# Moving the expert part's tiles in SBUF by unused tiles of 32 to 96 bytes, in a decoder layer on one Trainium2 core

## What is computed

```python
router_probs = softmax(x @ w_router)
gate_weights = softmax((x @ w_gating) / GATE_TEMP)
g = einsum('bsh,ehf->ebsf', x, w_gate)      # E=8 experts, H=256, F=1024
u = einsum('bsh,ehf->ebsf', x, w_up)
h = silu(g) * u
expert_out = einsum('ebsf,efh->ebsh', h, w_down)
cw = router_probs * gate_weights
cw = cw / (cw.sum(-1) + 1e-09)
out = einsum('ebsh,bse->bsh', expert_out, cw)
x = layernorm(x + out)
```

## The kernel before

| tile | before | rem. 256 | after | rem. 256 |
|---|---|---|---|---|
| xh, xl (tokens) | 57984, 72320 | 128 | same | 128 |
| wh0, wl0 | 86656, 98944 | 128 | 86720, 99008 | 192 |
| acc | 111232 | 128 | 111296 | 192 |
| wh1, wl1 | 127584, 139872 | 96 | 127744, 140032 | 0 |
| sil0, sil1, hf0, hf1 | 152160 to 158304 | 96 | 152320 to 158464 | 0 |
| hh0, hl0 | 160352, 176736 | 96 | 160544, 168736 | 32 |
| hh1, hl1 | 168544, 184928 | 96 | 176960, 185152 | 64 |
| xk | 193120 | 96 | 193344 | 64 |

## Time and profile before

### The profile page before, as it was taken

One profiled execution on the slowest core, in us unless ns is written; L12 is line 12 of the kernel. 1 busy time (PEld: TensorE's weight loads), 2 busy tenths in 40 slices (PEclk: granted clock), 3 DMA queues, 4 the chain that ended last, 5 costly groups with the idle time before them and its releaser, 6 DMA issues. The chain is left out here.

```text
span 1966.1 us, 25813 instructions
## 1 busy us (share of the span) xinstructions
PE 1807.1 (92%) x9624; PEld 1491.7 (76%) x9624; DVE 1329.3 (68%) x2421; ACT 842.5 (43%) x1327; POOL 2.6 (0%) x22
## 2 busy tenths in 40 slices
PE   2399999999999987888789999999999999999997
PEld 1277777777777775555579988989988889898986
DVE  6889999999999952899864444454444454454445
ACT  2466677666667733222243333232333232333333
POOL 0000000000000000000000000000000000000000
PEclk9689999999999998889779999999999999999999
DMA  3000001001001002112020101000000000002001
GB/s 107 0 27 17 6 27 38 6 6 43 17 12 48 1 0 66 64 31 60 10 74 33 33 1 33 33 32 32 32 0 32 32 32 32 32 2 67 1 1 38
DMA packets 35648, 56.98 MB, mean 29 GB/s; under 512 B 2997, under 2 KB 20850, under 8 KB 35058
## 3 DMA queue, kind: packets, MB, share of 16 engines
q1 hardware_dynamic: 35570, 55.95, 8.8%
HBM read 52.27 MB, written 3.67 MB: 28 GB/s over the span
## 5 line engine op out<-in xcount | busy, mean ns | idle before, releaser
L1424 DVE TENSOR_TENSOR hf<-sil,fbanks 128x512 f32<-128x512 f32 (+1 forms) x128 | 79.4, 621 | 338.1 <-PE fbanks L1593 278.7
L1532 ACT ACTIVATE sil<-fbanks 128x512 f32<-128x512 f32 (+1 forms) x128 | 69.6, 544 | 448.7 <-PE fbanks L1593 448.7
L1609 PE MATMUL fbank<-wl,hh 128*128 128x256 f32 x896 | 251.9, 281 | 0.0
L1609 PE MATMUL fbank<-wh,hl 128*128 128x256 f32 x896 | 251.8, 281 | 0.0
L1609 PE MATMUL fbank<-wh,hh 128*128 128x256 f32 x896 | 251.8, 281 | 0.0
L1424 DVE TENSOR_TENSOR hf<-sil,fbank 128x512 f32<-128x512 f32 (+1 forms) x128 | 79.6, 621 | 154.2 <-PE fbank L1593 147.0
L725 PE MATMUL pair<-wcv,kf 128*112 128x256 f32 x768 | 176.2, 379 | 0.0
L1609 PEld LDWEIGHTS fbank<-wl,hh 128*128 128x128 f32 x896 | 170.1, 190 | 2.1
L1609 PEld LDWEIGHTS fbank<-wh,hh 128*128 128x128 f32 x896 | 170.0, 190 | 2.0
L1609 PEld LDWEIGHTS fbank<-wh,hl 128*128 128x128 f32 x896 | 170.2, 190 | 0.0
L1431 DVE TENSOR_TENSOR hl<-hf,hh 128x512 fp32r<-128x512 f32 (+1 forms) x256 | 158.3, 618 | 0.0
(11 more groups left out here) (220 smaller groups left out, 3452.2 us busy)
## 6 DMA issues: line engine op xcount, KB each, us to landing
raw<-in_w_gate SPq DMA_DIRECT2D x16, 512.0 KB, 3.7
raw<-in_w_up SPq DMA_DIRECT2D x16, 512.0 KB, 4.7
raw<-in_w_down SPq DMA_DIRECT2D x16, 512.0 KB, 5.6
raw<-in_w_ck SPq DMA_DIRECT2D x4, 1024.0 KB, 4.9
wcv<-in_w_cv SPq DMA_DIRECT2D x4, 768.0 KB, 4.5
raw<-in_ctx_t SPq DMA_DIRECT2D x4, 750.0 KB, 5.3
ct<-in_ctx_t SPq DMA_DIRECT2D x4, 750.0 KB, 4.9
x<-in_x SPq DMA_DIRECT2D x4, 448.0 KB, 6.6
```

The source lines that it names most:

```text
L1424: dve.tensor_tensor(hf[i][:, 0:w], sil[i][:, 0:w], bank[2 * i + 1][:, 0:w], ALU.mult).then_inc(hf_ready, 1)
L1532: act.activation(sil[f % 2][:, 0:w], bank[2 * (f % 2)][:, 0:w], ACT.Silu).then_inc(sil_ready, 1)
L1609: ins = pe.matmul(bank[4 + 2 * (t % 2) + i // 2][:, (i % 2) * C:(i % 2 + 1) * C], a[t % 2][:, f, i * P:(i + 1) * P], m[h][:, DOWN + f * C: ...
```

## The change

Four tiles that nothing reads or writes are allocated between the others, and hl0 is allocated before hh1. Every instruction stays. With `gap_w0` (64 bytes) the weights of half 0 stand at +64 from the tokens by the remainder of 256, with `gap_w1` (96 bytes) those of half 1 at +128. `gap_h0` and `gap_h1` (32 bytes each) put hh0 and hl0 32 bytes past a multiple of 64 and hh1 and hl1 on one. Counting the loaded tile's remainder minus the streaming tile's:

| matmuls | before | after |
|---|---|---|
| gate and up, half 0 | 0 | +64 |
| gate and up, half 1 | -32 | +128 |
| down, half 0, even and odd steps | -32, -32 | +96, +128 |
| down, half 1, even and odd steps | 0, 0 | +32, +64 |

```diff
@@ -1283,11 +1283,15 @@
         top, total, rec = (sb(n, [P, 2 * TILES]) for n in ("ltop", "ltotal", "lrec"))
         cw = sb("cw", [P, E, TILES])
         cws, cwr = sb("cws", [P, TILES]), sb("cwr", [P, TILES])
+        sb("gap_w1", [P, 24])
         wh, wl = g["wh"] + [sb("wh1", [P, WH], F32R)], g["wl"] + [sb("wl1", [P, WH], F32R)]
         sil = [sb(f"sil{i}", [P, COLS]) for i in range(2)]
         hf = [sb(f"hf{i}", [P, COLS]) for i in range(2)]
-        hh = [sb(f"hh{i}", [P, FB, COLS], F32R) for i in range(2)]
-        hl = [sb(f"hl{i}", [P, FB, COLS], F32R) for i in range(2)]
+        sb("gap_h0", [P, 8])
+        hh, hl = ([sb(f"{n}0", [P, FB, COLS], F32R)] for n in ("hh", "hl"))
+        sb("gap_h1", [P, 8])
+        hh.append(sb("hh1", [P, FB, COLS], F32R))
+        hl.append(sb("hl1", [P, FB, COLS], F32R))
         xk = sb("xk", [P, TILES, C])
@@ -1654,6 +1658,7 @@
         rwkv_phase(nc, g, io)
         g["xh"], g["xl"] = (ctx.enter_context(nc.sbuf_tensor(n, [P, CB, N], F32R)) for n in ("xh", "xl"))
+        ctx.enter_context(nc.sbuf_tensor("gap_w0", [P, 16], FP32))
         g["wh"], g["wl"] = ([ctx.enter_context(nc.sbuf_tensor(n, [P, WH], F32R))] for n in ("wh0", "wl0"))
         g["acc"] = ctx.enter_context(nc.sbuf_tensor("acc", [P, TILES, C], FP32))
```

## The result

The changed kernel takes 1967.38 us (median of 20 runs, 1965.52 to 1972.71), the kernel before 1963.37 us (20 runs beside them, 1960.82 to 1969.80). The ratio is 1.0017, with a 95% interval of 1.0009 to 1.0024: slower by 0.17%, where 7 us less was forecast. 1967.4 us lies inside the range, on the wrong side of the time before.

What follows compares the result with a forecast made beforehand. TensorE's matmul pace was taken to bound the expert part. Terms of -7.2, +0.9, -2.4 and +1.8 us summed to -6.9, so 1964.2 became 1957.3 us, with a range of 1944 to 1970 us.

Steps and rivals of the forecast that it cites:

- What bounds the kernel: Expert part: its 941.6 us are TensorE's alone, shortened only by the pace at which matmuls follow each other.
- That the place of one operand against the other sets the pace: Expert matmuls: loaded tile's place against the streaming tile's sets the surcharge of 10 to 20 ns per matmul.
- That it is a cost of two reads at once: Expert matmuls: the next weights' load and the stream read SBUF together; the 10 to 20 ns surcharge is their mutual cost.
- the reading by remainder of 64: Gate, up and down: distances priced as multiples of 64 or off them, -6.9 us in sum; chance 0.42.
- The slower rival: Half 0 loses distance 0: gate/up at 233.3 ns, down 119.8 everywhere, +7.2 and +4.2 us, 1966 to 1976 us; chance 0.18.
- the bursts of six: First part's 256-column channel matmuls, 112 weights: 118 ns at 0, 114 at -128 (+128 by 256), 120 at +64; left out of sum.
- Nothing moves: Expert part: halves differ by something other than distance, such as region, so the time stays at 1964 us; chance 0.20.
- Down: Down matmuls: half 1's even steps gain 2.4 us, half 0's odd steps lose 1.8, the other steps keep their price.
- Part 3: Everything behind gap_w0 moves by 64 to 224 bytes; costed at nothing in the attention part and hidden in the expert part.
- the prediction's own sign: Rows up to 1011.7 us should keep their times within a microsecond or two, else the costing of moved tiles is wrong.

Runs made afterwards that it cites:

- zero_both: Kernel before with tiles moved so weights stand at distance 0 from the tokens and down at -32 in both halves; 1952.44 us, ratio 0.9947.
- w0_back: Changed kernel without gap_w0 and with gap_w1 of 40 elements, so half 0's weights return to distance 0 from the tokens; expert part 942.3 us.
- all_moved: Kernel before with all tiles 64 bytes further, distances by remainder of 256 as before, hl0 allocated before hh1; expert part 941.3 us.
- short_loads: Kernel before with 64 of 128 weight columns in the middle four of each six gate/up matmuls; 512 tokens took 228.9 and 232.1 ns (halves 0, 1).
- short_32: Kernel before with 32 of 128 weight columns in the middle four of each six gate/up matmuls; 512 tokens took 230.6 and 232.1 ns (halves 0, 1).
- the map: Table over several kernels that differ in tile places, weights -96 to +128 bytes from tokens; gate/up with 512 tokens 227.2 ns at 0, 234.1 at +96.
- zero_256: zero_both with gap_w1 of 72 elements in place of 8, so everything from wh1 on stands 256 bytes further; expert part 931.0 us.
- last_64: zero_both with the last 256 tokens 48 elements further in xh and xl, putting weights at +64 from them; 1951.11 us, ratio 0.9943.
- last_down_64: last_64 with hh and hl of both parities at +64 from the weights instead of -32; expert part 928.8 us.

## Why the prediction was wrong

*What bounds the kernel* held. The expert part is TensorE's alone, and its length moved the total one to one: +4.1 us gave +4.0 in the medians, and in zero_both -10.2 us (-9.3 in the second profile, with the later rise of the clock) gave -10.2.

*That the place of one operand against the other sets the pace* held, and is shown: w0_back, zero_both, all_moved. *That it is a cost of two reads at once* was argued only, and its plain form, a price for each column that the load reads, is refuted at 512 tokens by short_loads and short_32. Whether the start of a load has a part in it wasn't tried.

*The failed step is the reading by remainder of 64*: "The nearest reading is by remainder of 64, since 0 and -32 are the two classes that rows 5 tell apart." Two points were made into two classes, and +64 and +128 were priced by them. Of the twelve distances in the map nine cost 232 to 234 ns, and the kernel before had in half 0 the cheapest of all. Moving half 1 from -32 to another distance was worth 0.8 us instead of 7.2, and moving half 0 away from 0 cost 7.1 instead of nothing. Those two terms are 6.4 + 7.1 = 13.5 us of error; the 256-token steps gave back 2.3 us in half 0 and 0.6 in half 1, and down added 0.5, which leaves, but for rounding, the 11.0 us between -6.9 and +4.1. (The prediction's product 6.2 x 1152 is 7.1; its 7.2 is that of the unrounded paces.)

*The slower rival* came nearest: "0 against not 0 by a remainder over 64". Its +7.2 us for half 0 was measured as +7.1. Of its 11.4 us 4.1 came, since it had +4.2 us for down, where the sum of the four terms is -0.1, and nothing for the 256-token steps of half 0 (-2.3) and the 512-token steps of half 1 (-0.8). Nor is its rule exact, with -16 and -64 near 0. I gave it 0.18 because I set the bursts of six against it. The bursts had +128 as the fastest; in the steady stream +128 is among the slow ones in gate and up, and in down among the slowest (119.9 ns) in step 1. What bursts of six matmuls with 112 weights showed did not carry over to streams of 48 with 128.

*Nothing moves* is out by the paces, though the total came near it. By the Trainium skill (SBUF — State Buffer, SBUF: two separate sides) TensorE waits for nobody at the SBUF ports, and (TensorE: Matmul & The Clock Gate, Back-to-back issue gap) 2.5 ns lie between matmuls. That section gives the 2.5 ns for an isolated matmul, and says itself that a stream with weight loads goes at another pace; the prediction took them for the stream. These traces don't agree with 2.5 ns at any of the twelve distances: over the columns' time they have 13.9 to 20.8 ns at 512 tokens. What TensorE would wait for, they don't show.

*Down*: the forecast -0.6 us in all is near -0.1, from terms that were wrong by up to 2.0 us each. Part 3 put what moved in the first two parts at nothing. By the prediction's own sign, rows that keep their times up to 1011.7 us "within a microsecond or two", it would be wrong, since the expert part started 4.9 us earlier; but that start moved by 6.0 us between two executions of one kernel, so the sign can't tell. Part 3 agrees with the expert part's 4.1 us making up the whole difference; no experiment isolated it.

## What to carry to other kernels

Where TensorE is busy without a gap, read its pace from starts divided by counts, step by step, and not from the mean duration: the same instruction ran at 227 and 233 ns for a reason no group on the page shows. Two values at two places don't give the law between them. A few kernels that only move tiles give a table, since the pace of a stream is reproducible to 0.1 ns in one profile; they gave no law here either. Then put the loaded tile where the map is low for the streamed one (here a multiple of 256 bytes apart for 512 columns) and check each pair of tiles by itself, since the low lay elsewhere for down (-32) and for the 256-token steps.

## What the runs showed of the hardware

- fp32r matmuls of 512 columns at 2.4 GHz follow each other in 226.9 to 234.3 ns by the distance of the two operands in SBUF, of 256 columns in 113.5 to 120.5. At distance 0 a further 256 bytes change nothing (zero_256), and neither does a common shift of all tiles by 64 bytes (all_moved).
- The map has no slope: 0 is at 227.2, -8 at 233.3 and -16 at 228.5 ns.
- One distance (+64, 256 columns) can have two steady paces, 113.8 and 117.8 ns, and which one a step takes depends on the place of tiles that its own matmuls don't read (last_64 and last_down_64; the changed kernel and w0_back).
- Weight loads of a quarter of the columns beside four of six matmuls of 512 columns moved their mean pace from 227.1 to 230.6 ns in half 0 and from 233.3 to 232.1 in half 1.
- The clock granted to TensorE rose from 0.50 to 1.00 3.4 to 5.5 us into the expert part, in the profiles of before, after, w0_back and zero_both, and stayed there to the part's end.

What in the reads makes these prices stays open.
